# A recurrence of 64 steps: three of its four vector operations on whole rows in place of halves

## The reference, cut to what matters

```
b = (q * k).sum(-1) * SCALE                  # one number per token and head
a = -softplus(alpha).sum(-1)                 # likewise
vs, vl = sign(v), log(abs(v) + EPS)
def step(carry, inp):
    ln, nm, sg = carry
    ln = stable_lse(a_t + ln, b_t)
    dec = a_t[..., None] + nm
    new = b_t[..., None] + vl_t[:, None, :]
    m = maximum(dec, new)
    ssum = sg * exp(dec - m) + vs_t * exp(new - m)
    nsg = sign(ssum)                         # 0 counts as 1
    nm = m + log(abs(ssum) + EPS)
    y = (nsg * exp(nm - ln[..., None])).sum(-2)
```

## Time and profile before

| | |
|---|---|
| median of 3 runs | 2039.79 us (2038.75 to 2043.52) |
| profiled execution, its own time | 2044.84 us |
| its span | 2042.4 us |
| mean granted TensorE clock | 0.943 |
| TensorE busy | 1881.7 us, 92% |
| VectorE busy | 1333.6 us, 65% |
| ScalarE busy | 1124.4 us, 55% |
| GpSimd busy | 136.6 us, 7% |

### The profile page before, as it was taken

The page is one execution under the profiler, slowest core; times in us unless marked ns, Lnnn a source line. Parts: engine busy times, 40 slices in busy tenths (PEclk is TensorE's granted clock), DMA queues, the critical chain, the costliest instruction groups (busy, mean ns, idle before and its releaser), DMA issues. The chain is left out here.

```text
span 2042.4 us, 31431 instructions
## 1 busy us (share of the span) xinstructions
PE 1881.7 (92%) x10506; PEld 1501.4 (74%) x10506; DVE 1333.6 (65%) x2451; ACT 1124.4 (55%) x1864; POOL 136.6 (7%) x130
## 2 busy tenths in 40 slices
PE   7989985999997599999999999999968899889998
PEld 4667875999996578787878787878746667665664
DVE  4784546999996474636363545454528898878686
ACT  5762324888885354545454444444426666656663
POOL 0001000111110110000000000000000000002221
PEclk9999976999999799999999999999987988879999
DMA  6300042453424221101010101012040000020000
GB/s 235 108 32 1 1 161 90 150 205 128 178 89 165 93 71 34 51 16 51 15 51 15 51 15 51 15 51 82 16 141 42 1 1 1 1 88 1 1 21 21
DMA packets 22750, 129.80 MB, mean 64 GB/s; under 512 B 3601, under 2 KB 3857, under 8 KB 18962
## 3 DMA queue, kind: packets, MB, share of 16 engines
q1 hardware_dynamic: 17714, 112.59, 15.0%
q0 software_dynamic: 4960, 16.26, 2.4%
HBM read 116.51 MB, written 12.32 MB: 63 GB/s over the span
## 5 line engine op out<-in xcount | busy, mean ns | idle before, releaser
L116 PE MATMUL PS<-cT,qs 128*128 128x512 f32 x1152 | 298.4, 404 | 3.3 <-DVE qs L1697 2.2
L116 PE MATMUL PS<-pT,cN 128*128 128x512 f32 x1152 | 269.8, 392 | 1.7 <-DVE pT L1697 1.7
L116 PEld LDWEIGHTS PS<-cT,qs 128*128 128x128 f32 x1152 | 209.5, 188 | 52.6 <-issue 8.9
L116 PEld LDWEIGHTS PS<-pT,cN 128*128 128x128 f32 x1152 | 213.9, 188 | 45.0 <-DVE pT L1697 1.9
L116 PE MATMUL PS<-fw,xgT 128*128 128x384 f32 x1104 | 204.6, 340 | 5.7 <-DVE xgT L1244 5.7
L116 PEld LDWEIGHTS PS<-fw,xgT 128*128 128x128 f32 x1104 | 193.3, 190 | 9.3 <-DVE xgT L1244 6.3
L1692 DVE TENSOR_REDUCE nmax<-PS 128x1 f32<-128x512 f32 x128 | 87.8, 686 | 156.5 <-PE PS L116 156.4
L1244 DVE TENSOR_TENSOR fw<-W,fw 128x1536 fp32r<-128x1536 f32 x92 | 159.4, 1755 | 22.8 <-ACT fw L1164 22.8
L116 PE MATMUL PS<-xT,ws 128*128 128x512 f32 x576 | 155.1, 422 | 15.1 <-PEq L2599 8.7
L1597 ACT ACTIVATE qp<-PS 128x512 f32<-128x512 f32 x96 | 57.4, 598 | 187.9 <-PE PS L116 187.9
L1164 ACT ACTIVATE fw<-W 128x1536 fp32r x92 | 134.4, 1488 | 33.2 <-issue 33.2
(11 more groups left out here) (289 smaller groups left out, 3406.8 us busy)
## 6 DMA issues: line engine op xcount, KB each, us to landing
W<-in_fc SPq DMA_DIRECT2D x8, 3072.0 KB, 11.0
cT<-in_ctxT SPq DMA_DIRECT2D x16, 768.0 KB, 4.3
raw_pj<-in_proj SPq DMA_DIRECT2D x8, 1536.0 KB
ct_in<-in_ctxT SPq DMA_DIRECT2D x16, 768.0 KB, 4.3
cn_in<-in_ctxN SPq DMA_DIRECT2D x16, 768.0 KB
W<-in_w SPq DMA_DIRECT2D x2, 4096.0 KB, 13.1
routed_y<-y POOLq DMA_DIRECT2D x22, 256.0 KB
W<-in_w SPq DMA_DIRECT2D x5, 1024.0 KB, 7.1
```

What stands on the lines that cost most here:

```text
L116: mm = nc.tensor.matmul(out, lhs(m, s), rhs(n, s), start=(opens and (s, m, n) == terms[0]), stop=((s, m, n) == terms[-1]))
```

## The change

`s`, `ep` and `sg` become one operation on 512 columns each. Each waits for both halves of what it reads and raises its semaphore by 2. The new state and `ear` stay in halves; both halves of the new state now wait for the whole `sg`. In `weights`, `al` and `be` become the two rows of one tile `coefs`, `eal` and `ebe` those of one tile `small`, and one product on 2 x 8 columns takes the place of two in the chain. Nothing moves to another step or queue.

```diff
-        t1, t2, eA, eB, rd, al, be, eal, ebe = (...)
+        t1, t2, eA, eB, rd = (sbuf(n, [P, S]) for n in ("t15", "t25", "eA5", "eB5", "rd5"))
+        coefs, small = sbuf("coefs5", [P, 2, S]), sbuf("small5", [P, 2, S])
+        (al, be), (eal, ebe) = ([tile[:, n, :] for n in range(2)] for tile in (coefs, small))
...
-                    ch.link(nc.vector.tensor_scalar(eal[:, now(c)], al[:, now(c)], EPS, None, ALU.mult))
-                    ins = nc.vector.tensor_scalar(ebe[:, now(c)], be[:, now(c)], EPS, None, ALU.mult)
+                    ins = nc.vector.tensor_scalar(small[:, :, now(c)], coefs[:, :, now(c)], EPS, None, ALU.mult)
...
                         ve.wait_ge(bv_sb, BASE + t + 1)
-                        for h, cols in enumerate(HALVES):
-                            ve.wait_ge(r_sb, BASE + 2 * t + h + 1)
-                            nc.vector.scalar_tensor_tensor(s_[:, cols], old[:, cols], al[:, t:t + 1], bv[:, t % 2, cols],
-                                                           ALU.mult, ALU.add).then_inc(s_sb, 1)
+                        ve.wait_ge(r_sb, BASE + 2 * t + 2)
+                        nc.vector.scalar_tensor_tensor(s_[:, :], old, al[:, t:t + 1], bv[:, t % 2, :],
+                                                       ALU.mult, ALU.add).then_inc(s_sb, 2)
...
-                        for h, cols in enumerate(HALVES):
-                            ve.wait_ge(ear_sb, BASE + 2 * t + h + 1)
-                            nc.vector.tensor_tensor(ep[:, cols], ear[:, cols], ebv[:, t % 2, cols],
-                                                    ALU.max).then_inc(ep_sb, 1)
+                        ve.wait_ge(ear_sb, BASE + 2 * t + 2)
+                        nc.vector.tensor_tensor(ep[:, :], ear[:, :], ebv[:, t % 2, :], ALU.max).then_inc(ep_sb, 2)
...
-                        for h, cols in enumerate(HALVES):
-                            ve.wait_ge(s_sb, BASE + 2 * t + h + 1)
-                            ve.wait_ge(ep_sb, BASE + 2 * t + h + 1)
-                            nc.vector.scalar_tensor_tensor(sg[:, cols].bitcast(U32), ...).then_inc(sg_sb, 1)
+                        ve.wait_ge(s_sb, BASE + 2 * t + 2)
+                        ve.wait_ge(ep_sb, BASE + 2 * t + 2)
+                        nc.vector.scalar_tensor_tensor(sg[:, :].bitcast(U32), ...).then_inc(sg_sb, 2)
                         ve.wait_ge(y_mm, BASE + t + 1)
                         for h, cols in enumerate(HALVES):
-                            ve.wait_ge(sg_sb, BASE + 2 * t + h + 1)
+                            ve.wait_ge(sg_sb, BASE + 2 * t + 2)
                             nc.vector.tensor_tensor(new[:, cols], s_[:, cols], sg[:, cols], ALU.add).then_inc(r_sb, 1)
```

More of the change, by code:

```diff
@@ L1832, in decayed_attention_layer @@
         mx, dn = sbuf("mx5", [P, 1 + S]), sbuf("dn5", [P, 1 + S])
-        t1, t2, eA, eB, rd, al, be, eal, ebe = (sbuf(n, [P, S]) for n in ("t15", "t25", "eA5", "eB5", "rd5", "al5", "be5",
-                                                                       "eal5", "ebe5"))
+        t1, t2, eA, eB, rd = (sbuf(n, [P, S]) for n in ("t15", "t25", "eA5", "eB5", "rd5"))
+        coefs, small = sbuf("coefs5", [P, 2, S]), sbuf("small5", [P, 2, S])
+        (al, be), (eal, ebe) = ([tile[:, n, :] for n in range(2)] for tile in (coefs, small))
         bv, ebv = sbuf("bv5", [P, 2, D]), sbuf("ebv5", [P, 2, D])
@@ L2238, in _ @@
                             add_out(c - 1)
-                        for h, cols in enumerate(HALVES):
-                            ve.wait_ge(s_sb, BASE + 2 * t + h + 1)
-                            ve.wait_ge(ep_sb, BASE + 2 * t + h + 1)
-                            nc.vector.scalar_tensor_tensor(sg[:, cols].bitcast(U32), s_[:, cols].bitcast(U32), SIGN_BIT,
-                                                           ep[:, cols].bitcast(U32), ALU.bitwise_and,
-                                                           ALU.bitwise_or).then_inc(sg_sb, 1)
+                        ve.wait_ge(s_sb, BASE + 2 * t + 2)
+                        ve.wait_ge(ep_sb, BASE + 2 * t + 2)
+                        nc.vector.scalar_tensor_tensor(sg[:, :].bitcast(U32), s_[:, :].bitcast(U32), SIGN_BIT,
+                                                       ep[:, :].bitcast(U32), ALU.bitwise_and,
+                                                       ALU.bitwise_or).then_inc(sg_sb, 2)
                         ve.wait_ge(y_mm, BASE + t + 1)
                         for h, cols in enumerate(HALVES):
-                            ve.wait_ge(sg_sb, BASE + 2 * t + h + 1)
+                            ve.wait_ge(sg_sb, BASE + 2 * t + 2)
                             nc.vector.tensor_tensor(new[:, cols], s_[:, cols], sg[:, cols], ALU.add).then_inc(r_sb, 1)
```

## The result

The changed kernel took 2050.6 us (2049.91 to 2052.39, 6 runs) against 2040.84 us for the kernel before on the same chip (6 runs): a ratio of 1.0049, 95% interval 1.0036 to 1.0062. It is 10 us slower, where I forecast 2.7 us and gave 2048.5 as the upper end.

The account below looks back on a forecast made before the run. TensorE was taken to pace most of groups 1 to 6, VectorE the rest; 0.50 + 0.155 + 1.11 - 0.08 + 0.95 + 0.05 = +2.7 us on the 2039.79 us median gave 2042.5 us, range 2035 to 2048.5.

Parts of the forecast that it names:

- The price of a whole operation: VectorE's 512-column operations cost 0.60 us if the next doesn't need them, 0.72 if it does; 0.062 more for `s`.
- the overlap of halves that is lost: On VectorE, half 0 of the next operation needs only half 0 of the last; a half takes up 0.335 us, lasting 0.42.
- without other work: Step 6 and steps 0 to 6 of group 7, new state to new state: 2.99 us against 2.80, +0.19.
- the upper bound: Highest total, +6.7 us: dependent joins take 0.10 us, not 0.03, up to 0.2 us a step on some 20 uncovered steps.
- the sum: Costs added over groups 0 to 7 of the scan: +2.7 us in total, 0.13%.
- The second half of `ear`: `ep` now waits for both halves of ScalarE's `ear`, so it can't start before 1.55 us after the new state.
- The wait for the K projection: VectorE's wait at the products of step 3, groups 1 to 6, about 0.3 us each, would shrink to about nothing.
- TensorE's cover: TensorE paces most of groups 1 to 6, with VectorE 0.3 us ahead, hiding VectorE's added cost there.
- the stretch from step 4 to the products: Step 4 to the products of the next step 3: VectorE grows 0.36 us against 0.3 of waiting, costed at nothing.
- The clock (0.24): Rival, chance 0.24: TensorE's granted clock falls in longer waits at steps 3 and 4; +7.3 us, 2047.1 us.
- the fourth case: Rival, chance 0.07: all six periods run in 33.8 us at a good TensorE clock, 9 us less; 2033.5 us.
- Fewer instructions win: Rival, chance 0.12: dependence between VectorE operations costs nothing, fewer instructions gain; -4.5 us, 2035.3 us.

Follow-up runs that it names:

- Run 2: Changed kernel with its whole operations raising semaphores by 1 and, of two waits, the one that ends last written first: 1.0000 to the kernel before, 2041.02 us.
- run 7: Unneeded value projections repeated in TensorE's waits: kernel before 0.9986, changed kernel as it is 1.0060, changed kernel raising by 1 with the late wait first 0.9967.
- runs 1: Changed kernel with its three whole operations raising their semaphores by 1 in place of 2, order of waits unchanged: 1.0047 to the kernel before, 2050.27 us.
- the mix: Kernel before with small products as one and ep whole only in steps 1, 5 and 7: 0.9991; with repeated value projections 0.9969, 2034.92 us.

## Why the prediction was wrong

**The step that failed** is "The price of a whole operation". I took 0.72 us for an operation that the next one needs, 0.03 of it for the join, from L2125 and L2127. L2127 waits for one semaphore and carries it itself. The operations of the scan wait for two, and in the changed kernel they raise by 2: their joins cost 0.13, 0.14 and 0.10 us. The sizes of the operations were right (0.75, 0.69, 0.69), so was the overlap of halves that is lost. Run 2 gives the joins the form of L2127, and its step takes 2.94 us against my 2.99. A warning was in the kernel before: the queue shows 64 or 128 wait instructions at the lines of `ep` and `sg`. In the steps without other work they lay beside the other half and VectorE had no gap. That they would come to stand alone is what I did not ask.

One place where such a wait stood alone was even among my rows. The 0.10 us from the end of a half of `ear` to `ep` I took for the signal between two engines, and built the upper bound on it. In the trace a separate wait of 21 ns, line 2225, stands in that gap, at 1589.55. In run 2, where `ep` carries this wait itself, the same signal from ScalarE costs 0.03.

**The upper bound** had 0.10 us a join, but on "some 20 steps that nothing covers". The step lengths show it in nearly all:

| step | forecast | measured (before, after) |
|---|---|---|
| without other work | +0.19 | +0.40 (2.80, 3.20) |
| 0 | +0.085 | +0.40 (3.94, 4.34) |
| 4 | +0.085 | +0.38 (3.40, 3.78) |
| 5, group 2 | -0.035 | +0.12 (4.68, 4.80) |
| 7, group 2 | -0.235 | -0.03 (4.79, 4.76) |
| 3, group 0 | +0.085 | +0.20 (4.61, 4.81) |
| 1 and 2, group 0 | +0.37 | +0.48 (8.96, 9.44) |

**Point by point.** From the first new state to step 4 of group 0 the sum had +0.54, the trace has +1.05. For the six periods it had 1.27 and got 5.4; behind them 0.92 against 2.6. The second half of `ear` does set the start of `ep`, 1.58 us after the new state where I had 1.55. The wait for the K projection shrank to nothing, as the prediction asked of its own reading. TensorE's cover is real, and its size and place were wrong too. I costed the stretch from step 4 to the products at nothing, with 0.3 us of cover against 0.36. By the table the steps of a group grew by 1.95 us together, 11.7 in six periods, of which 5.4 passed. The rest came out of VectorE's waits: the one for the K projection (1.9 us before, none after), where I had put the cover, and that of `ep` for `ear` at steps 1 and 2 (14.7, 10.7), where I had put none. Behind this second wait ScalarE waits for TensorE's A projection, 8.4 us before and 6.0 after; the table load is only a part of it.

**The rivals.** The clock (0.24) is refuted as the cause of the loss: in the six periods it was 0.82 against 0.84, and with the clock up the changed kernel is as slow (run 7). As a fact it is large, 7 us in six periods, and the fourth case was right that there was time to be had. "Fewer instructions win" is refuted by the step lengths. The rule of the Trainium skill behind it ("VectorE: DVE Perf Modes", section "The DRAIN you can't avoid"), by which a semaphore between chained operations costs nothing extra, is too coarse here. It compares operations with and without a semaphore, and no run here leaves one out; but runs 1 and 2 have the same operations and the same semaphores, and differ by 0.2 us a step and 9 us in all through which instruction carries the wait. The advice to minimise the count of operations stands in the same page's section "Rules for kernel authors"; the changed kernel has some 200 operations fewer and is the slower one.

## What to carry to other kernels

Before two halves are made one, ask which wait the next operation then stands behind alone, and look in the engine's queue for what carries it: with two waits, write the one that ends last first, and raise the semaphore by 1. Here a whole operation gained a little where other work stood behind it (step 5 of group 2: 4.68 us, 4.59 in the mix) and lost where the next one needed it (2.80 us a step, 2.94 with the best waits). Where an engine with a granted clock waits, try a filler in the wait before moving work into it: here the filler gained and the move lost.

## What the runs showed that I had not expected

- The order in which two waits are written is worth 0.2 us a step here (3.15 to 2.94 us), and in every run the operations that raise a semaphore by 2 carry no wait of their own: their waits stand in a separate instruction, 50 ns in place of 21 in the changed kernel.
- Adding some 70 matmuls to six periods made them 7 us shorter (211.75 to 204.80 us), while the granted clock rose from 0.84 to 0.97. Moving an out projection into a wait, with the pieces that depend on it, made the kernel 9 us slower, while the clock fell from 0.82 to 0.77 over the scan.
